# Adding the residual and the bias of an attention projection on TensorE: an identity product in place of two elementwise additions

## The reference

```
q  = layernorm(x) @ Wq + bq                    # 1024 tokens, 16 heads of 16
kv = ctx @ Wkv + bkv                           # 1024 keys
q, k, v fake-quantised to 8 bits (scale of each row, v: of each column)
attn = softmax(q . k / 4), quantised to 255 steps of its largest
out  = attn @ v                                # (1024, 256)
x    = x + (out @ Wp + bp)                     # <- the sum that the change moves
x    = x + (layernorm(x) @ ternary(W).T + b)   # the step behind it
```

## Time and profile before

| what | us |
|---|---|
| runs | 308.97, 312.82, 312.83 |
| profiled execution | 310.26 |
| its span, first to last instruction | 308.5 |
| busy, PE (matmul) | 229.9 (75%) |
| busy, VectorE (DVE) | 256.1 (83%) |
| busy, ScalarE (ACT) | 205.9 (67%) |
| busy, GpSimd (POOL) | 172.6 (56%) |
| row maxima on VectorE, 128 of 1.218 | 152.4 |
| exponentials on ScalarE, 128 of 1.20 | 153.2 |

### The profile page before, as it was taken

The page is one execution under the profiler, slowest core; times in us unless marked ns, Lnnn a source line. Parts: engine busy times, 40 slices in busy tenths (PEclk is TensorE's granted clock), DMA queues, the critical chain, the costliest instruction groups (busy, mean ns, idle before and its releaser), DMA issues.

```text
span 308.5 us, 6467 instructions
## 1 busy us (share of the span) xinstructions
PE 229.9 (75%) x2256; PEld 161.0 (52%) x2286; DVE 256.1 (83%) x393; ACT 205.9 (67%) x354; POOL 172.6 (56%) x352
## 2 busy tenths in 40 slices
PE   4996749668657975787877787878776877777882
PEld 3543637456544762155554555555554555555761
DVE  2453989967869689989999999999999999999661
ACT  1100023434487735899999999999998999998410
POOL 2270244526660301377776767777777677777554
PEclk9999997959765796579999999999999999999998
DMA  7926000005999808979979989989899999899311
GB/s 244 316 103 154 3 1 0 2 0 110 191 180 185 154 2 156 200 141 166 167 149 154 157 163 163 134 180 163 123 187 155 121 188 155 156 154 151 61 64 68
DMA packets 133808, 41.07 MB, mean 133 GB/s; under 512 B 126352, under 2 KB 132880, under 8 KB 133776
## 3 DMA queue, kind: packets, MB, share of 16 engines
q1 hardware_dynamic: 131680, 37.24, 68.1%
q0 software_dynamic: 768, 2.10, 1.9%
q10 hardware_dynamic: 1328, 1.32, 1.3%
HBM read 5.25 MB, written 2.10 MB: 24 GB/s over the span
## 4 chain that ended last, share of the span: by engine, by line
ACT 23%; POOL 20%; DVE 18%; issue 18%; PE 12%; DMA 8%; POOLq 0%; ACTq 0%; DVEq 0%
ACT ctxT L640 11%; ACT ctx L640 9%; POOL gates L475 9%; POOL ebias L464 4%; DMA ksplit<-in_x 3%; PE ps L1171 3%; DVE nmax L979 3%; POOL scratch L408 2%; PE ps L1405 2%; DMA xs<-scratch 2%; POOL rstd L414 2%; DMA ksplit<-ctxT 1%; POOL out L501 1%; PE ps L1313 1%; PE ps L1295 1%
## 5 line engine op out<-in xcount | busy, mean ns | idle before, releaser
L979 DVE TENSOR_REDUCE nmax<-ps 128x1 f32<-128x1024 f32 x128 | 152.4, 1218 | 6.5 <-PE ps L1313 5.3
L1313 PE MATMUL ps<-keysT,kv 128*128 128x512 bf16 x226 | 75.2, 408 | 38.7 <-ACT ctx L640 24.5
L475 POOL CAST gates<-ksplit 128x512 int16<-128x512 uint8 x124 | 75.7, 611 | 10.9 <-DMA ksplit<-ctxT 2.4
L640 ACT ACTIVATE ctx<-ps,ebias,qscale 128x1024 uint8<-128x1024 f32 x64 | 76.7, 1202 | 5.4 <-POOL ebias L464 5.3
L640 ACT ACTIVATE ctxT<-ps,ebias,qscale 128x1024 uint8<-128x1024 f32 x64 | 76.5, 1200 | 0.8 <-POOL ebias L464 0.7
L464 POOL TENSOR_SCALAR ebias<-nmax,qscale 128x1 f32<-128x1 f32 x128 | 33.9, 265 | 40.8 <-DVE nmax L979 36.7
L1340 PEld LDWEIGHTS ps<-identb 128*128 128x128 bf16 x428 | 32.7, 99 | 24.9 <-issue 1.1
L1340 PE MATMUL ps<-identb 128*128 128x128 bf16 x428 | 41.8, 221 | 0.9 <-POOL gates L475 0.9
L1313 PEld LDWEIGHTS ps<-keysT,kv 128*128 128x128 bf16 x256 | 15.1, 99 | 50.5 <-ACT ctx L640 26.8
L533 ACT COPY hT<-ps 128x256 f32<-128x256 f32 x11 | 4.1, 372 | 47.0 <-PE ps L1163 47.0
L1347 PE MATMUL ps<-vals,gates 128*128 128x16 f16 x512 | 22.3, 170 | 0.0
(11 more groups left out here) (190 smaller groups left out, 356.0 us busy)
## 6 DMA issues: line engine op xcount, KB each, us to landing
keysT<-zeros SPq DMA_DIRECT2D x4, 512.0 KB, 8.1
ctx<-in_ctx SPq DMA_DIRECT2D x2, 512.0 KB, 4.8
ksplit<-in_x ACTq DMA_DIRECT2D x1, 1024.0 KB, 10.8
xs<-scratch SPq DMA_DIRECT2D x1, 1024.0 KB, 5.6
wkv_s<-in_L_xattn_Wkv SPq DMA_DIRECT2D x1, 512.0 KB, 7.9
ksplit<-ctx SPq DMA_TRANSPOSE x32, 3.8
ksplit<-ctxT SPq DMA_TRANSPOSE x32, 3.8
bkv_b<-in_L_xattn_bkv ACTq DMA_DIRECT2D x1, 256.0 KB, 11.2
```

The lines of the kernel that those rows point to most:

```text
L475: g.tensor_copy(byteT[:, w % PT, part, :, :], rawT[:, w % PAIRS, part, :].bitcast(U8).rearrange("p b (q j) -> p b j q", j=2)).then_inc(unp ...
L640: a.activation(probs, s_in, ACT.Exp, bias=ebias[:, u % 4:u % 4 + 1], scale=qscale[:, t, u:u + 1], accum_out=lsum[:, t, u:u + 1]).then_inc( ...
L979: v.tensor_reduce(nmax[:, u % 4:u % 4 + 1], score_banks(k, u), AX.X, ALU.max, negate=True).then_inc(max_ready, 1)
L1313: last = m.matmul(ps[:, bank + b, :], qT[:, t, u // 2, :], keysT[:, u % 2, u // 2, 512 * b:512 * b + 512], start=True, stop=True)
```

## The change

TensorE forms the whole sum in the PSUM region of the projection. A new function `residual` multiplies the identity with the residual tile (128 x 256, float32), then a row of ones with the row bp, and the two halves of the projection accumulate upon them. ScalarE copies the sum into xs behind its exponential of head 15. VectorE's addition and GpSimd's two halves of the bias go. The projection moves from steps 11 and 12 to 12 and 13, and `residual` takes step 11; fillers are left out in the steps 9, 11, 12 and 13. In the tail `residual` stands before the last projection in PE's list, and the copy of the sum behind the copy of unit 2 in ScalarE's.

```
-BIAS_AT = 9
-PROJECT_AT = 11
-ADD_AT = 15
+PROJECT_AT = 12
+RESIDUAL_AT = 11
+MOVE_AT = 15
...
 GpSimd, attention:
-                    if u in (BIAS_AT, BIAS_AT + 1):
-                        part = slice((u - BIAS_AT) * P, (u - BIAS_AT + 1) * P)
-                        g.tensor_tensor(xs[:, t, part], xs[:, t, part], bp_b[:, part], ALU.add).then_inc(x3b_ready, 1)
...
 ScalarE:
+            def move_sum(t):
+                act.wait_ge(proj_full, t + 1)
+                a.copy(xs[:, t, :], ps[:, PV_BANKS[t % 2], D:2 * D]).then_inc(x3_ready, 1)
...
+                    if u == MOVE_AT and not first_tile(t):
+                        move_sum(t - 1)
...
             copy_att(NT - 1)
-            for i in range(2, len(UNITS)):
+            copy_h4(2)
+            move_sum(NT - 1)
+            for i in range(3, len(UNITS)):
                 copy_h4(i)
...
 VectorE:
-            def add_projection(t):
-                dve.wait_ge(proj_full, t + 1)
-                dve.wait_ge(x3b_ready, 2 * t + 2)
-                v.tensor_tensor(xs[:, t, :], ps[:, PV_BANKS[t % 2], D:2 * D], xs[:, t, :], ALU.add).then_inc(x3_ready, 1)
...
-                    if u == ADD_AT and not first_tile(t):
-                        add_projection(t - 1)
...
-            add_projection(last_tile)
             dve.wait_ge(x3_ready, NT)
...
 PE:
+            def residual(t):
+                pe.wait_ge(attT_ready, t + 1)
+                total = ps[:, PV_BANKS[t % 2], D:2 * D]
+                m.matmul(total, identf[:, :], xs[:, t, :], start=True, stop=False)
+                m.matmul(total, onesf[0:1, :], bp_b[0:1, :], start=False, stop=False)
...
 project:
-                                start=(c == 0), stop=(c == C - 1))
+                                start=False, stop=(c == C - 1))
...
-                    if u in (TURN_AT, PROJECT_AT, PROJECT_AT + 1) and not first_tile(t):
+                    if u in (TURN_AT, RESIDUAL_AT, PROJECT_AT, PROJECT_AT + 1) and not first_tile(t):
                         if u == TURN_AT:
                             att_turn(t - 1)
+                        elif u == RESIDUAL_AT:
+                            residual(t - 1)
                         else:
                             project(t - 1, u - PROJECT_AT)
...
             pe.wait_ge(vals_ready, 1)
+            pe.wait_ge(ld_b, 48)
...
             h4_turn(2)
+            residual(NT - 1)
             project(NT - 1, 0)
```

More of the change, by code:

```diff
@@ L265, in build @@
         turned = [sem(f"turned{i}") for i in range(PAIRS)]
-        linv_ready, att_ready, x3b_ready = sem("linv_ready"), sem("att_ready"), sem("x3b_ready")
+        linv_ready, att_ready = sem("linv_ready"), sem("att_ready")
         attT_full, attT_ready, proj_full, x3_ready = sem("attT_full"), sem("attT_ready"), sem("proj_full"), sem("x3_ready")
```

## The result

The changed kernel takes 320.08 us (median of 4 runs, 317.32 to 320.31), the kernel before 311.98 (four runs, the fourth 311.13): a ratio of 1.0257, interval 1.0164 to 1.035. It is slower, by 8.1 us between the medians, where 4.55 were forecast. The profiled executions, 320.16 and 310.26 us, differ by 9.9.

| mark | before | after | added since the mark above |
|---|---|---|---|
| first row maximum of the loop | 119.44 | 120.56 | 1.12 |
| ScalarE's first copy in the loop | 155.78 | 156.94 | 0.04 |
| its last copy in the loop | 277.50 | 281.45 | 2.79 |
| its copy of the last tile | 295.56 | 304.19 | 4.68 |
| scatter of unit 2 | 299.93 | 309.81 | 1.25 |

A forecast was written before the change was run, and what follows sets the result against it. A ring of three score buffers and ScalarE, equally tight, were taken to bound the loop. 2.5 - 0.35 + 1.5 + 0.9 = +4.55 us gave 314.8 from the profile or 317.4 from the median; 316 was named, range 312 to 320.

The forecast's parts named there:

- the 2% to which I had given 0.17: Whole kernel: the chance given to a slowdown beyond two per cent, over 319.1 us, was 0.17.
- the third rival: Loop step 11: weight loads of the new products not hidden, each pass 0.40 us; +9.6 us in all, chance 0.16.
- the sum of +4.55: Loop and tail: 2.5 - 0.35 + 1.5 + 0.9 us, the forecast's total slowdown.
- The ring: Attention loop: three score buffers make scores of head u+3 wait for exponential u, 3.62 us per three heads; delays add.
- The addition, 0.25 us a tile: Loop, VectorE: removing its addition frees at most 0.25 us a tile before exponential 0 of the next tile.
- The copy, 0.25: Loop, ScalarE: copying the sum behind the exponential of head 15 displaces the next exponential by 0.25 us a tile.
- walked through: Loop, one tile followed from scores 15, 0.43 us late: next tile some 0.41 us later, six tiles +2.5 us.
- GpSimd's halves, -0.35 us: Loop, GpSimd: dropping its two halves of the bias saves 0.05 us a tile over 7 tiles.
- PE's products, the first failed step: Loop step 11, PE: identity product and bias row take 0.44 us each, 0.88 together; the step grows by 0.44.
- The 1.19 us of steps 12 and 13: Loop, PE: each of these steps lasts 1.19 us with a projection call, so lateness from step 11 isn't recovered there.
- The tail, the second failed step: Tail: VectorE waits 2.0 us for ScalarE's copy of the seventh sum; 0.5 hidden by unpacking, +1.5 us on the chain.
- The second part of the tail: Tail, PE: identity product and bias of the last tile stand ahead of the last projection, nothing hides them; +0.9 us.

The follow-up runs named there:

- experiment 3: Changed kernel with the bias row added as identity times the bias on all 128 partitions, not a one-partition product: 318.03 us, ratio 1.0244.
- experiment 4: Changed kernel with one new call a step: identity product in step 10, projection in 11 and 12, 128-partition bias in 13: 315.18 us, ratio 1.0148.
- experiment 6: Kernel before without VectorE's addition in the loop (projections of tiles 0 to 6 not added): 310.36 us, ratio 0.9994.
- experiment 5: Kernel before plus a spare ScalarE copy of 128 x 256 behind the exponential of head 15, tiles 1 to 7: 311.26 us, ratio 0.9996.
- experiment 8: Changed kernel, loop products spread one call a step, last tile as in the kernel before, VectorE's tail wait split four and seven: 311.17 us, ratio 1.0016.
- experiment 2: Changed kernel with 56 filler transposes on PE in place of 8 ahead of the tail's first transposes: 317.81 us, ratio 1.0221.
- experiment 1: Changed kernel with VectorE's tail wait split: four sums before the first statistics, all seven before those of tiles 4 to 6: 313.96 us, ratio 1.0111.
- experiment 7: Kernel before plus the two new products alone in step 11, results overwritten, projection in 12 and 13, additions kept: 317.92 us, ratio 1.0209.

## Why the prediction was right in kind and short in size

Direction and places were right: slower, in step 11, ahead of VectorE's statistics, and ahead of the last projection. The time, 320.08 us, came out on the upper edge of the range of 312 to 320, above the forecast's own 313 to 319, and beyond the 2% to which I had given 0.17. That the range reaches so far is owed to the third rival and not to the sum of +4.55; the rival's +9.6 came close to the 9.9 of the profiles by luck, since its reason held for one of its two calls and the rest was the clock, which it did not have.

- **The ring** held. A tile is longer by what scores 15 are late: 0.32 us late gives 20.34, 0.62 gives 20.64, none gives 20.02 (experiments 3 and 4). Work that is late for the ring isn't made up.
- **The addition, 0.25 us a tile**: 0.22 (experiment 6). **The copy, 0.25**: 0.26 after the change, and 0.03 where the gap is still there (experiment 5). The two cancel, as walked through (experiments 4 and 8). By the estimate from the Trainium skill's figures ("ScalarE: Activation LUTs", What ACT_TABLE_LOAD costs) it would have been 0.31; the traces bear out the row, with 0.25 before the change and 0.26 after it.
- **GpSimd's halves, -0.35 us**: from maximum 10 to its bias are 1.31 us (196.07 to 197.38) where 1.37 were; in the tiles (20.01 to 20.04 in experiment 4) it can't be seen.
- **PE's products, the first failed step.** "I take 0.44, as for 128 partitions, since the moved columns are the same" was wrong. The bias row took 0.62 us and both calls 1.15 in place of 0.88; scores 15 were 0.62 late, not 0.43. Six tiles at 0.62 are 3.7 us, not 2.5. The third rival named the mechanism, loads that aren't hidden, but gave it to both calls; it holds for the one-partition call only, at 0.31 a pass (experiment 3). The 1.19 us of steps 12 and 13 was misread too: it was the pace of the exponentials that free the score buffers, and step 12 now takes 203.37 - 202.31 = 1.06. The lateness stays all the same, because exponential 0 follows ScalarE, as the walk had it.
- **The tail, the second failed step.** "1.5 are on the chain, which from there goes through PE without a gap": VectorE waited 2.0 us as said, and half a us was hidden, but the walk took PE's clock as given. PE's wait of 3.00 us was followed by 6.0 us at the lower clock, worth 2.70 us (experiment 2); the wait itself came to 1.98, where 1.5 were forecast (experiments 1 and 2). Counted from the last copy in the loop, the statistics start 2.22 us later than before (scores 15 of the last tile are 0.62 late, not 0.43) and the transposes 2.51, because the two normalisations between them take 1.30 us in place of 1.03. They take 1.30 in the eight profiles in which GpSimd's unpacking begins 0.07 or 0.08 us ahead of them, and 1.03 in the two in which it begins 0.14 or 0.15 behind; why is not shown. No rival had the clock in it, though the kernel's list holds fillers at just that place.
- **The second part of the tail**: 1.25 us for 0.88, the same one-partition call.

In steady tiles and tail that is 3.7 + 4.68 + 1.25 = 9.6 us. The marks show 2.79 for the loop, because the profiled execution of before had longer tiles among its steady ones (20.74 and 20.22; first 20.64), the one after fewer (first 21.31). These long tiles ran at a granted clock of 1.00, and what made them long is open. In other kernels the clock has a part: the tiles of 22.1 us and more in experiments 2, 3, 5, 6 and 7 have a mean granted clock of 0.92 or 0.93.

## What to carry to other kernels

Where buffers form a ring, cost an edit by how late it makes the next link, step by step, and not by an engine's busy share; work that fits between two links is free, the same work in one step isn't. When an operation moves to another engine, look at who waits for it in the next stage: the queue that did it itself never waited. And where a new wait leaves TensorE idle, count the clock too.

## What the runs showed of the hardware

A float32 product with one partition, among products with 128, costs more than one with 128: 0.62 against 0.43 us for 256 columns, and the product ahead of it takes 0.10 more. Its loads are not longer (182 ns, against 190 for 128 partitions), but they start later. In all eight calls the first load begins 0.31 us after the start of the product ahead, and the second 0.11 us after the start of the call's own first product; with 128 partitions (experiment 3) a load begins within 0.01 us of the start of the running product. The loads of the next 128-partition product are late as well, after 0.33 us of idle time. Whether the form itself or the change of form on both sides makes them late, no run here tells. The Trainium skill ("TensorE: Matmul & The Clock Gate", Step-by-step: what each phase is for) says that a load's time goes by columns and not by partitions, which these loads bear out. It says too that PE pulls loads ahead of running products when the row groups don't conflict or the load goes to the background weight buffer: the loads with 128 partitions agree, at 0.01 us, and no run here shows which condition the late ones missed.

VectorE's row maxima, 1.22 us each, start 1.13 us apart when nothing holds them (3.49 us for three, after 0.57 of waiting). So with a busy share of 98% (19.56 of 20.02 us) VectorE could still start a maximum every 1.13 us, where ScalarE needs 1.20 for an exponential.
